# The search of a graph kernel ahead of its attention groups, in two PSUM banks; every gather ahead of every scatter

## The reference

```
h = relu(layernorm(x));  x = x + messages(h, src, dst, ...)     # segment_sum over dst
h = relu(layernorm(x));  x = x + attention(h, src, dst) @ Wout  # softmax over the edges of one dst
```

## Time and profile before

| | us |
|---|---|
| median of 3 runs (lowest, highest) | 1321.79 (1319.41, 1324.59) |
| the profiled execution, its own time | 1320.73 |
| its span in the trace | 1318.9 |
| busy: PE, DVE, ACT, POOL | 813.2, 973.2, 848.4, 833.2 |
| 196 gathers of sums (L703), 196 scatters (L710) | 209.0, 221.5 |

### The profile page before, as it was taken

The page is one execution under the profiler, slowest core; times in us unless marked ns, Lnnn a source line. Parts: engine busy times, 40 slices in busy tenths (PEclk is TensorE's granted clock), DMA queues, the critical chain, the costliest instruction groups (busy, mean ns, idle before and its releaser), DMA issues.

```text
span 1318.9 us, 16579 instructions
## 1 busy us (share of the span) xinstructions
PE 813.2 (62%) x5136; PEld 641.7 (49%) x5136; DVE 973.2 (74%) x1734; ACT 848.4 (64%) x2015; POOL 833.2 (63%) x796
## 2 busy tenths in 40 slices
PE   0278878778788788788441112657565666777640
PEld 0267767667677677677230001344334434555430
DVE  6598988889888988885688777546634575999850
ACT  1377787878878777874645453576556755888720
POOL 6777766767767766600477430467676776878875
PEclk9878788798788787887555556687767867999975
DMA  5121112122212211102433231001110100000000
GB/s 130 20 64 43 41 40 45 35 54 67 64 25 55 65 45 40 31 21 74 178 113 81 78 91 50 32 10 38 37 39 16 33 10 11 10 10 9 10 10 7
DMA packets 40667, 60.50 MB, mean 46 GB/s; under 512 B 17361, under 2 KB 31077, under 8 KB 40324
## 3 DMA queue, kind: packets, MB, share of 16 engines
q1 hardware_dynamic: 12216, 46.86, 11.0%
q0 software_dynamic: 25184, 12.32, 5.9%
q10 hardware_dynamic: 3180, 0.26, 0.2%
HBM read 40.33 MB, written 19.37 MB: 45 GB/s over the span
## 4 chain that ended last, share of the span: by engine, by line
PE 30%; DVE 23%; POOL 14%; ACT 13%; issue 8%; DVEq 5%; DMA 4%; POOLq 0%; SPq 0%
PE sums L1091 12%; POOL out_dram L710 9%; DVE h1d_or_products L1418 5%; ACT below L913 4%; POOL x_rows L677 3%; PE tens L1081 3%; DMA out_dram<-xin 2%; ACT h1d_or_products L822 2%; PE tens L1197 2%; PE turnB L1220 2%; DVE halves_or_steps L1411 2%; POOL agg_or_stacks L703 2%; DMA xin<-in_x 2%; PE turnB L1067 2%; ACT features_or_rows L976 2%
## 5 line engine op out<-in xcount | busy, mean ns | idle before, releaser
L710 POOL DMA_INDIRECT out_dram<-agg_or_stacks,scatter_index x196 | 221.5, 1130 | 136.4 <-ACT agg_or_stacks L983 79.2
L703 POOL DMA_INDIRECT agg_or_stacks<-run_sums,sum_row_index x196 | 209.0, 1066 | 97.9 <-issue 55.8
L677 POOL DMA_INDIRECT x_rows<-in_x,src_index x196 | 197.9, 1010 | 93.4 <-issue 50.3
L677 POOL DMA_INDIRECT x_rows<-in_x,dst_index x196 | 200.0, 1021 | 63.2 <-issue 63.2
L1418 DVE TENSOR_TENSOR h1d_or_products<-tens,hid 128x768 f32<-128x768 f32 x168 | 156.4, 949 | 14.9 <-PE tens L1085 14.5
L1091 PE MATMUL sums<-h1d_or_products,ident 128*128 128x192 f32 x896 | 151.7, 328 | 0.0
L1091 PEld LDWEIGHTS sums<-h1d_or_products,ident 128*128 128x128 f32 x896 | 145.0, 190 | 0.0
L1157 PE MATMUL sums<-one_column,halves_or_steps 128*128 128x1 f16 x166 | 30.7, 185 | 175.5 <-ACT below L913 136.9
L976 ACT ACTIVATE features_or_rows<-stack_turned,is_last 128x132 f32<-128x132 f32 x196 | 85.8, 521 | 82.0 <-DVE stack_turned L1741 82.0
L1157 PEld LDWEIGHTS sums<-one_column,halves_or_steps 128*128 128x128 f16 x166 | 18.9, 114 | 197.0 <-ACT below L913 149.6
L913 ACT ACTIVATE below<-sums,bias_of_src 128x196 bf16<-128x196 f32 x166 | 68.8, 419 | 55.7 <-PE sums L1159 55.4
(11 more groups left out here) (306 smaller groups left out, 2445.0 us busy)
## 6 DMA issues: line engine op xcount, KB each, us to landing
src_everywhere<-src_by_columns SPq DMA_DIRECT2D x14, 896.0 KB
xin<-in_x SPq DMA_DIRECT2D x27, 449.5 KB
out_dram<-xin SPq DMA_DIRECT2D x27, 449.5 KB
x_rows<-in_x,src_index POOLq DMA_INDIRECT x196, 2.7
x_rows<-in_x,dst_index POOLq DMA_INDIRECT x196, 2.9
run<-run_sums SPq DMA_DIRECT2D x1, 3136.0 KB, 11.4
agg_or_stacks<-run_sums,sum_row_index POOLq DMA_INDIRECT x196, 2.5
out_dram<-agg_or_stacks,scatter_index POOLq DMA_INDIRECT x196, 2.1
```

Source lines behind the costliest of these rows:

```text
L677: nc.gpsimd.indirect_dma_start(xs[:, t, side, :], None, x, bass.IndirectOffsetOnAxis(ap=idx[:, t:t + 1], axis=0)).then_inc(s_gath[g % LEAD ...
L703: nc.gpsimd.indirect_dma_start(aggr[:, t, :], None, rs, bass.IndirectOffsetOnAxis(ap=ridx[:, t:t + 1], axis=0)).then_inc(s_rsg[g % LEAD2], 16)
L710: nc.gpsimd.indirect_dma_start(out, bass.IndirectOffsetOnAxis(ap=sidx[:, t:t + 1], axis=0), aggr[:, t, :], None, bounds_check=N - 1, oob_i ...
```

## The change

- The search of chunks 5 to 13 stands in nine steps ahead of the attention groups, always in two banks, seven pairs at a time. Step j searches chunk 5 + j; steps 0 to 6 also hold one dense slice and one block each, steps 7 and 8 none (step 7 the last `dst_scale`). The thirds, the halves and the one-bank form are gone, and with them all searching within `group2`.
- SyncE issues the broadcast of a step's next chunk ahead of that step's store and load.
- GpSimd gathers all 196 columns, with a wait for `s_ridx` once a chunk and none on `s_cnt`, then waits for the dense stores, then scatters all 196.
- The semaphores of the gathers are one to a group, 28 in place of 12.

```diff
+    C1 = 5
+    STEPS = NCHUNK - C1
+    D2 = len(SLICE1) + 2
+    PER = -(-(ND - D2) // STEPS)
 # SyncE
+            for j in range(STEPS):
+                if C1 + j + 1 < NCHUNK:
+                    sp.wait_ge(s_S, C1 + j + 1)
+                    spread_src(C1 + j + 1)
+                for d in slices_of(j):
+                    store(d)
+                    if d + 2 < ND:
+                        load(d + 2)
 # GpSimd
-            def gather(g):
-                if past(g, LEAD2 - 1):
-                    pool.wait_ge(s_bc, g - LEAD2 + 1)
-                for t in range(g * GA, (g + 1) * GA):
-                    c, i = t // CT, t % CT
-                    if i == 0:
-                        pool.wait_ge(s_ridx, c + 1)
-                    elif i % 2 == 0 and c + 1 < C2:
-                        pool.wait_ge(s_cnt, (c + 1) * PAIRS + i // 2)
-                    nc.gpsimd.indirect_dma_start(
+            for t in range(T):
+                c, i = t // CT, t % CT
+                if i == 0:
+                    pool.wait_ge(s_ridx, c + 1)
+                nc.gpsimd.indirect_dma_start(
...
             for g in range(NG):
                 scatter(g)
-                if fits(g + LEAD2):
-                    gather(g + LEAD2)
 # ScalarE
+            for j in range(STEPS):
+                for i, d in enumerate(slices_of(j)):
+                    dense_square(d)
+                    if i == 0 and j < NBLK:
+                        dst_square(j)
+                    dense_deviation(d)
+                if j < NBLK:
+                    dst_deviation(j)
+                compare(C1 + j, range(PAIRS))
 # TensorE
-            for j in range(3 * (C2 - C1)):
-                search(C1 + j // 3, THIRDS[j % 3])
+            for c in range(C1, NCHUNK):
+                search(c, range(PAIRS))
 # VectorE
+            for j in range(STEPS):
+                for i, d in enumerate(slices_of(j)):
+                    dense_sums(d, dsum_p)
+                    v.drain()
+                    dense_centre(d, dsum_p)
+                    if i == 0 and j < NBLK:
+                        dst_centre(j)
+                    if i == len(slices_of(j)) - 1 and 0 < j <= NBLK:
+                        dst_scale(j - 1)
+                    if i == 0:
+                        if j > 0:
+                            decode(C1 + j - 1)
+                        search_steps(C1 + j)
+                    dense_variance(d)
+                    if i == len(slices_of(j)) - 1 and j < NBLK:
+                        dst_variance(j)
+                    dense_scale(d, drec_p)
+                    dense_add(d)
+                if len(slices_of(j)) == 0:
+                    decode(C1 + j - 1)
+                    search_steps(C1 + j)
+                    if j == NBLK:
+                        dst_scale(j - 1)
+            decode(NCHUNK - 1)
...
-            def group2(g, b, found):
-                if found and b == 0:
-                    search_steps(C2 + g // 2)
+            def group2(g, b):
```

More of the change, by code:

```diff
@@ L82, in build_gnn, with slices_of @@
     NBLK = NG // NB
-    SLICE2 = range(len(SLICE1) + 2, len(SLICE1) + 2 + NBLK)
-    assert NBLK * NB == NG and SLICE2[-1] == ND - 1
+    C1 = 5
+    STEPS = NCHUNK - C1
+    D2 = len(SLICE1) + 2
+    PER = -(-(ND - D2) // STEPS)
+    assert NBLK * NB == NG and NBLK < STEPS
+    def slices_of(j):
+        return range(D2 + j * PER, min(D2 + (j + 1) * PER, ND))
     MARKS = (0, 10, 18, NG - 2, NG)
     assert all(m in SLICE1 for m in MARKS[1:-1])
-    C1 = 5
-    C2 = C1 + 2
     LEAD1 = 4
     AHEAD = 23
-    LEAD2 = 12
-    NPS = NCHUNK - C2
     F1 = FEAT + 1
-    assert ND == 2 * NP and 1 < NPS < NP - 1
     ctx = ExitStack()
@@ L452, in build_gnn @@
         s_back = sem("running_sums_reloaded")
-        s_rsg = [sem(f"sums_gathered{i}") for i in range(LEAD2)]
+        s_rsg = [sem(f"sums_gathered{i}") for i in range(NG)]
         s_vb = sem("src_spread")
@@ L713, in scatter @@
                     ).then_inc(s_osc, 16)
-            for g in range(LEAD2):
-                gather(g)
             pool.wait_ge(s_dout[0], 16 * (ND // 2))
@@ L1156, in search @@
                         of = steps[:, tile * P:(tile + 1) * P]
-                        nc.tensor.matmul(parts[:, j:j + 1], of, one_col[:], start=True, stop=True)
+                        nc.tensor.matmul(parts_at[i % 2][:, i // 2, j:j + 1], of, one_col[:], start=True, stop=True)
                         nc.tensor.matmul(bank[:, j * T:(j + 1) * T], of, dhi[:], start=True, stop=False)
@@ L1235, in group2 @@
                     sum_heads(g - 1)
-                if len(pairs) > 0:
-                    search(C2 + g // 2, pairs)
             pe.wait_ge(s_gbd, 16 * 8)
@@ L1586, in decode @@
                 v.drain()
-                if past(c, C1 - 1):
-                    v.scalar_tensor_tensor(found_f[:, 0], parts_one, float(T), found_f[:, 0], ALU.mult, ALU.subtract)
-                else:
-                    for i in range(2):
-                        at = by_pair[:, 0:(PAIRS + 1 - i) // 2, i, :]
-                        v.scalar_tensor_tensor(at, parts_at[i][:, 0:(PAIRS + 1 - i) // 2, :], float(T), at, ALU.mult,
-                                               ALU.subtract)
+                for i in range(2):
+                    at = by_pair[:, 0:(PAIRS + 1 - i) // 2, i, :]
+                    v.scalar_tensor_tensor(at, parts_at[i][:, 0:(PAIRS + 1 - i) // 2, :], float(T), at, ALU.mult,
+                                           ALU.subtract)
                 v.drain()
@@ L1793, in group2 @@
                     source_rows(g + 2, b)
-                if found and b == 1:
-                    decode(C2 + g // 2)
             dve.wait_ge(s_dv, NBLK)
@@ L1807, in _ @@
             for k in range(NP):
-                group2(2 * k, 0, k < NPS)
-                group2(2 * k + 1, 1, k < NPS)
+                group2(2 * k, 0)
+                group2(2 * k + 1, 1)
             weigh(NG - 1, 1)
```

54 lines of the change are left out of this document (11 added, 43 removed).

## The result

| | before | after |
|---|---|---|
| median of 4 runs each, us | 1320.6 | 1223.1 (1220.54 to 1224.88) |
| ratio, 95% interval | | 0.926 (0.922 to 0.930) |
| the profiled execution, its own time, us | 1320.73 | 1220.54 |
| its span, us | 1318.9 | 1218.7 |

The forecast was 1227 us, with 1212 to 1236 for its own case and 1207 to 1250 for all. A repeat on another chip (`after_again`) gave a median of 1223.91 us and 0.925 (0.919 to 0.930). In the profile after, line 692 is the gather, 699 the scatter, 709 the fix rows, 1725 the scan, 1561 the decode, 1739 the product, 970 `take_out`.

A forecast was written before the change was run, and what follows sets the result against it. GpSimd was taken to set the end, fed slowly by groups with search. 736.4 + 160 gathers + 8 slice stage + 2 memsets + 252 scatters + 54 scans = 1212.4, plus 11.8 tail: span 1224.2, median 1227 us, range 1207 to 1250.

The forecast's parts named there:

- The end is GpSimd's, from the second chunk on: GpSimd's gathers and scatters set the end; from 665 us, chunk 1's first gather, it never waits for a decode.
- The slice stage: Gathers beside the slice steps lose time to VectorE: 1.1 us for each of seven new steps, 8 us.
- The rival of three losses a step: Each slice step costs GpSimd three losses (steps, slice's add, block's add): 9 us more, 1236 us; chance 0.08.
- The scans: In the groups, 28 VectorE scans each cost a GpSimd DMA 1.93 us: 54 us.
- The sum: GpSimd's terms added from 736.4 us give 1212.4 us for the start of the fix rows' scatter.
- The tail: From the fix rows' scatter to the end of the span: 11.8 us, taken from the old kernel.
- The margin: First group's rows are ready about 877 us, gathers end at 913: the search may end 35 us late free.
- A sign of being wrong that was set too tight: GpSimd's gathers over 1.4 us apart would show the queue or VectorE slowing them; 1.25 to 1.35 expected.
- The rule on SBUF: VectorE instructions with two SBUF inputs contend with GpSimd; slice's and block's adds would each cost a gather too.
- late groups: Rival: longer buffer rounds delay the search, so scatters wait for rows: 1234 us, or 1252 at 27 us a step; chance 0.07.
- lower level: Rival on the groups without TensorE's full clock: rows ready at 1294, end 1315 us, no real gain; chance 0.04.
- jam: Rival: 128 unpaced gathers in a row jam their DMA queue, each dearer at issue, up to 1387 us; slower has chance 0.03.

The follow-up runs named there:

- The two delays: Changed kernel with 14 or 36 extra VectorE memsets ahead of the first group: 1223.62 us (0.926) and 1277.38 us (0.969).
- one-bank version: Changed kernel with the search products of chunks 5 to 13 in one bank, still ahead of the groups: 1227.73 us, 0.930.
- experiment 5: Three versions of the changed kernel with the group's long scan cut in pieces, one with the exponential in PSUM: 1176.94, 1175.57 and 1192.79 us.
- search_only_b: Changed kernel with GpSimd's old order, scatters by turns with gathers twelve groups later: 1333.45 us, 1.011; on the first chip 0.998.
- gathers_only: Kernel before, its search unchanged, with all 196 gathers in one run ahead of the scatters: 1.060, from two executions.
- decay_cut: Changed kernel with the long scan in three pieces (512, 512, 32 columns) over a smaller exponential in SBUF, numerators laid out by feature: 1175.57 us, 0.889.
- late_36b: Changed kernel with 36 extra VectorE memsets, drains between, ahead of the groups: 1277.38 us, 0.969.
- scan_halves: Changed kernel with the scan of 1056 columns cut in two of 528, exponential and layout unchanged: 1192.79 us, 0.905.

## Why the prediction was right

Its steps, each against its rows:

- **The end is GpSimd's, from the second chunk on.** Right. One wait of 4.29 us at 657, then none; the kernel before lost 4.4 us in the same place, in two waits (2.48 and 1.96). The two delays and the one-bank version show it by intervention.
- **The start.** Not a term of the sum, and the largest difference of all: the phase of the messages, which the change doesn't touch, ended 7.8 us earlier in this execution (657.28 for 665.05). In the repeat it ended 7 us later than in this one (first gather at 642.86, fix rows at 1215.79). Most of it is one wait of GpSimd for the store of the running sums: 77.0 us in the kernel before and in the repeat, 71.9 in this execution. It is the spread of executions, not the change, and it is why an execution of 1220.5 stood beside a forecast of 1226.
- **The slice stage.** Forecast: 8 us, and 2 for the memsets. From the 69th gather (730.29) to the first scatter are 181.5 us; less 128 x 1.25 and 11.7 lost to scans leaves 9.8. The total was right; its parts weren't. The memsets cost nothing. The five slice steps in this stretch cost 1.8 us each and the two bare chunks 0.6 each, where the forecast had seven at 1.1. The rival of three losses a step named the right instructions (steps, slice's add, block's add), but they cost in full only where a gather starts just inside them. The 54 gathers ahead of it took 73.0 us in place of 71.4.
- **The scans.** Forecast 54 us. The six that met gathers cost 11.7 and the 22 that met scatters 42 (21 of 1.93 and the last of 1.2): 54. Right, and experiment 5 then took most of it away.
- **The scatters.** 196 x 1.29 is right. Not in the forecast: one pause of 2.97 us ahead of the 114th scatter, 2.7 more than any other.

```profile
1090.93 0.98 POOL L699 DMA_INDIRECT out_dram<-agg_or_stacks,scatter_index  x1 [2.97 <-issue]
```

- **The sum.** 1212.4 - 7.8 + 1.6 + 2.7 = 1208.9 for the fix rows; the row has 1209.29. The 1.6 are the first 54 gathers.
- **The tail.** Forecast 11.8, measured 9.4 (1218.7 less 1209.29). With GpSimd's old order it is 11.8 to 11.9 in all three executions profiled (1325.6 less 1313.72 in `search_only_b`), with all gathers first 9.4 to 9.5 in all eleven, also with the old search (`gathers_only`). So it goes with GpSimd's order, not with the search; why, the traces don't show. The repeat began as late as the kernel before and its span was 1225.3 for a forecast of 1224.2: that close a hit is partly luck, since the pause (2.7 more) and the tail (2.4 less) were both unforeseen and cancel.
- **The search's end** at 829 for 835 to 847, of which 7.8 is the start; the steps took the lower of the two lengths, 16.1. **The margin** was 49 us at the first scatter (take_out at 862.03, scatter at 911.79) for a forecast of 35. The first product came 3 us early once the start is taken off (842.91 + 7.8 for 854), the group's own way took 19 us for 23, and the gathers ended later than forecast by 1.6 and by two more scans, 4. The margin at the end, 39.5, is what counts, and the forecast hadn't worked that one out, though its numbers had it (1212 less 1183 is 29).
- **A sign of being wrong that was set too tight.** The prediction is wrong, it says, if the gathers stand over 1.4 us apart, and it gives 1.25 to 1.35 for them. From the 69th on they stood 1.42 apart on average (181.5 us for 128). No queue did this: the plain ones are 1.25 apart and the rest is the losses to VectorE, 21.5 us. The prediction's own terms gave 1.39 (160, 8, 2 and four scans over 128), so the sign would have stood at its edge in any case.
- **The rule on SBUF.** The row of the slice's add (719.17, 0.93 lost) and the scan in PSUM (nothing lost) are what the Trainium skill, "SBUF — State Buffer", section "Who interferes with whom", has for two SBUF inputs against one. The trace agrees. The instruction of 717.90 costs a gather nothing though it has two inputs, and its second one, `small`, is a PSUM bank (`small = pb("small")` in the kernel, where `pb` makes PSUM tensors). Whether the second operand is small doesn't matter: the product `dcen<-run,is_last` near the end of the groups repeats a small operand that lies in SBUF, and a scatter that starts in it loses 0.45 us (1.43 in place of 0.98). The steps, with one SBUF input and an output of f16, cost 0.5 to 0.9. The rule of two inputs doesn't speak of them; the same section of the Trainium skill counts `tensor_scalar`, which they are, among the instructions that can contend with GpSimd under conditions. That these conditions are met here, no run shows.

```profile
1145.25 0.96 DVE L1794 TENSOR_TENSOR dcen<-run,is_last 128x784 f32<-128x784 f32 x1
```
```profile
1145.64 1.43 POOL L699 DMA_INDIRECT out_dram<-agg_or_stacks,scatter_index  x1 [0.30 <-issue]
```

The rivals: no wait for rows in the scatters (no late groups), a granted clock of 1.00 in the groups (no lower level), plain gathers 1.25 apart with 128 in a row beside broadcasts and slices (no jam).

## What to carry to other kernels

A queue that is worked in order has two times, what its work takes and when each piece may start; to start a producer earlier pays only if the queue's order is changed to use it, and the reverse, so look for the other half before you judge either alone. When an engine is bound, sum its instructions first, then look for the long ones among equal rows and put each beside the other engine's row of that moment: here 54 us stood in 28 rows that were three times as long as their neighbours. Cutting one VectorE instruction in two gave back 31 us of it, and cutting it in three, with a smaller exponential and another layout, 48. Margin is to be worked out at the end of the program as well as at the first meeting.

## What the runs showed that I had not expected

- **Two engines fall into step.** With gathers beside them VectorE's groups took 10.78 us (873.52 to 884.31 between two scans), with scatters 10.94. The scatter's own period is 7 x 1.287 + 1.93 = 10.94: VectorE is held too, at a copy of 128x4 just ahead of the scan, which takes 0.28 in place of 0.12. The copy starts 0.70 us into a scatter of 0.98 and ends with it; one that starts 0.61 in takes 0.37, and one 0.19 to 0.38 in takes its 0.12 (21 times in `decay_cut`). So a scatter holds VectorE's copy only in its last 0.3 to 0.4 us, and each scan then starts at the same phase of the next scatter, 0.23 us ahead of it, where the loss is nearly the largest. Rows of the changed kernel and of `late_36b`, where GpSimd is idle at that moment:

```profile
949.24 0.28 DVE L1749 COPY run<-run 128x4 f32<-128x4 f32 x1
```
```profile
939.69 0.12 DVE L1749 COPY run<-run 128x4 f32<-128x4 f32 x1
```

  In `scan_halves` the step is 8 x 1.287 + 0.83 = 11.13, measured 11.14. That it's the copy that locks them is read from the rows; no run took it away.
- **Which instructions of VectorE hold up a gather**, over the 196 gathers of the trace after. A gather that starts inside one of these loses what is left of it, less 0.1 to 0.2: the add of a slice (0.17 to 0.93 in eight cases), the add of a block (0.20 to 0.80 in five), the steps to f16 (0.17 to 0.90 in eight), the group's long scan. A gather that starts up to 0.42 ahead of the steps is held too (0.56 to 0.76 in five). Nothing is lost to reductions, to memsets, and to two-input instructions with one operand in PSUM, however long: a gather or a scatter started inside L1423 9 times, inside L1411 7 times, inside L1733 (1.75 us long) 28 times, and inside the scans of 196 columns in L1630 13 times. All four read `small`, a PSUM bank. The ten traces that are not of the first chip draw the same line: two SBUF inputs cost, one in PSUM doesn't. Five gathers that started within 0.04 us of the start of an add or of the long scan got through without loss; all others that had more than 0.35 us of an add, the steps or the scan of 1056 before them lost time.
- **A pause of about 3 us** (2.96 to 3.75) in the run of scatters, once in each of the eleven executions profiled with all gathers first, on all chips, and always ahead of the 114th scatter: at 1050.77 us in `decay_cut`, at 1477.04 in `gathers_only`. So it hangs on the place in the order and not on the time. With the old order (the kernel before, `search_only`, `search_only_b`) no step between two of these DMAs that waits for nothing is above 0.31 us, the one ahead of the 114th scatter included. Its cause is open, as that of the tail is.
